# A two-lane attention GRU on one core: increments accumulated in PSUM, a bf16 score product for the shift, and DVE summing the exponentials

## The reference, cut to what matters

```python
def step(h, x_t):
    score = tanh([h ; enc] @ W_att)          # 77 x 128
    attn = softmax(score @ V_att)            # over the 77 context rows
    inp = [x_t ; attn @ enc]
    gz, gr, gh = split(inp @ Wi + b)
    rz, rr, rh = split(h @ Uh)
    z, r = sigmoid(gz + rz), sigmoid(gr + rr)
    hh = tanh(gh + r * rh)
    h_new = z * h + (1 - z) * hh
x = x + all h_new                            # x_t is layernorm(x)
```

## Time and profile before

| | us |
|---|---|
| median of 3 executions (4578.97 to 4592.61) | 4579.9 |
| span of the profiled execution, first to last instruction | 4575.7 |
| the profiled execution's own time | not given beside its span |
| recurrence in it, first to last write of h | 256.0 to 2283.5 |

### The profile page before, as it was taken

How to read it: one execution, slowest core, us unless ns; L and a number is a source line. 1 busy time by engine, 2 the same in 40 slices (tenths; PEclk the granted TensorE clock), 3 DMA queues, 4 the chain that set the end, 5 groups by cost and what they waited for, 6 DMA issues and landing times. The chain is left out here.

```text
span 4575.7 us, 82192 instructions
## 1 busy us (share of the span) xinstructions
PE 4041.4 (88%) x25247; PEld 2348.8 (51%) x25308; DVE 2805.4 (61%) x13508; ACT 2308.3 (50%) x6560; POOL 948.4 (21%) x4509
## 2 busy tenths in 40 slices
PE   7889999999999999999899999778888888888868
PEld 2367777777777777777733334322333333333222
DVE  3466666666666666666654454546666666666534
ACT  5355565555555555555533334214555555555423
POOL 0323333333333333333331000300000000100002
PEclk9999999999999999999999999758888888888879
DMA  0100000000000000000001000011111111111100
GB/s 9 56 2 2 2 2 2 2 2 2 2 2 2 2 2 2 2 2 2 6 31 37 1 1 1 22 57 45 45 57 45 57 57 45 57 52 49 33 30 5
DMA packets 48838, 94.48 MB, mean 21 GB/s; under 512 B 11296, under 2 KB 31792, under 8 KB 48144
## 3 DMA queue, kind: packets, MB, share of 16 engines
q1 hardware_dynamic: 48400, 89.22, 6.0%
HBM read 72.88 MB, written 15.39 MB: 19 GB/s over the span
## 5 line engine op out<-in xcount | busy, mean ns | idle before, releaser
L939 PE MATMUL ps<-g_h,w_p 128*128 128x128 f32 x4096 | 918.2, 306 | 0.0
L2280 ACT ACTIVATE t_ex<-ps 128x1024 f32<-128x1024 f32 (+1 forms) x480 | 471.8, 1021 | 571.8 <-PE ps L2227 558.1
L939 PEld LDWEIGHTS ps<-g_h,w_p 128*128 128x128 f32 x4096 | 616.7, 190 | 0.0
L935 PE MATMUL ps<-g_h,w_p 128*128 128x77 f32 x2048 | 456.5, 304 | 174.5 <-DVE g_h L1009 145.9
L2375 DVE TENSOR_REDUCE t_ncol<-ps 128x1 f32<-128x512 f32 x768 | 486.6, 685 | 154.6 <-PE ps L2200 154.0
L1005 DVE SCALAR_TENSOR_TENSOR g_used<-g_encg,g_e 128x77 f32<-128x77 f32 x3072 | 550.3, 230 | 0.0
L975 ACT ACTIVATE g_th<-ps 128x77 f32<-128x77 f32 x1024 | 241.4, 236 | 535.5 <-PE ps L935 535.5
L1051 POOL TENSOR_SCALAR g_z<-g_tzr 128x1 f32<-128x1 f32 x1024 | 194.7, 190 | 1363.0 <-ACT g_tzr L984 1363.0
L935 PEld LDWEIGHTS ps<-g_h,w_p 128*128 128x128 f32 x2048 | 304.5, 188 | 310.3 <-DVE g_h L1009 295.5
L956 PE MATMUL ps<-g_th,g_vrep 128*128 128x77 f32 x2048 | 456.6, 305 | 0.0
L1014 DVE TENSOR_REDUCE g_ntop<-ps 128x1 f32<-128x77 f32 x1024 | 244.1, 238 | 338.2 <-PE ps L956 337.3
(11 more groups left out here) (481 smaller groups left out, 6910.3 us busy)
## 6 DMA issues: line engine op xcount, KB each, us to landing
t_qst<-t_turn_q SPq DMA_DIRECT2D x288, 96.0 KB
t_kst<-t_turn_k SPq DMA_DIRECT2D x144, 96.0 KB
t_turn_q<-t_part SPq DMA_DIRECT2D x24, 384.0 KB, 2.5
t_turn_k<-t_part SPq DMA_DIRECT2D x12, 384.0 KB, 3.3
t_wf<-in_t_wf SPq DMA_DIRECT2D x6, 514.5 KB, 5.5
m_experts<-in_experts SPq DMA_DIRECT2D x1, 3072.0 KB, 12.7
t_wa<-in_t_wa SPq DMA_DIRECT2D x6, 448.0 KB, 3.4
t_wx<-in_t_wx SPq DMA_DIRECT2D x6, 448.0 KB, 4.2
```

Source lines behind the costliest of these rows:

```text
L935: M(att[c], w["att_h"], h[t % 2][:, c:c + 1].broadcast_to([P, S]), start=False, stop=True, skip_group_check=True).then_inc(*st.sem("att", c))
L939: return M(G[c][:, g], weights, h[t % 2][:, c:c + 1].broadcast_to([P, P]), start=False, stop=last, skip_group_check=True)
L2280: A(ex[0:kw, slot[pf, c, l, n]], ps[0:kw, at:at + 2], ACT.Exp, scale=SCALE).then_inc(*st.sem(f"{pf}e{n}", c))
```

## The change

- PE's operand is no longer h but its increment dh. The attention sum (`att`) and the gate sums (`gates`) are not opened anew at each step: they stay in PSUM, and each step adds W times dh to all 128 columns of a gate at once. Column t of the bank, which was filled with `gx` of 128 tokens by float32 identity products (`fill`), then holds the gate of token t. Once in 128 steps the banks are opened again from the full h (`hist`).
- r's and z's products both stand ahead of `scores`, the candidate's behind; the bf16 opening products are gone.
- `rough` is a new single bf16 product: the upper halves of tanh's float32 values times V in bf16. `top` takes the maximum from it, while exp still reads the float32 `score`.
- exp loses its accumulator output. DVE gets `sum`, a reduction of e over 77 columns, waits for it before the reciprocal, and `hm` moves behind `zr`.
- `update` makes dh = (hh - h) * (1 - z) on DVE. POOL keeps 1 - z and adds dh to the history, and drops z, z * h, the save and the splitting. DVE adds the whole history to x at the end.

```diff
...
-        gx = sb("gx", [P, B, T, 3])
+        gx = sb("gx", [P, B, 3, T])
...
-        gxs = sb("gxs", [P, 3, B, T, 3], BF16)
-        encs = sb("encs", [P, 3, B, S], BF16)
+        zero = sb("zero", [P, 1])
...
-        h = [sb(f"h{i}", [P, B]) for i in range(2)]
+        vrepb = sb("vrepb", [P, P], BF16)
+        hist = sb("hist", [P, B, T + 1])
+        dh = [sb(f"dh{i}", [P, B]) for i in range(2)]
...
+        SPAN = P
+        att = [ps[:, 4 * c, 0:S] for c in range(B)]
+        score = [ps[:, 4 * c + 1, 0:S] for c in range(B)]
+        rough = [ps[:, 4 * c + 3, 0:S] for c in range(B)]
+        upper = [th[:, c].bitcast(BF16).rearrange("p (s h) -> p s h", h=2)[:, :, 1] for c in range(B)]
+
+        gates = [ps[:, 4 * c + 2, 0:3 * SPAN].rearrange("p (g n) -> p g n", n=SPAN) for c in range(B)]
+        plain = [ps[:, 4 * c + 2, 3 * SPAN:3 * SPAN + 1] for c in range(B)]
...
-                def open_att(c):
-                    for i in range(3):
-                        M(att[c], identb[:], encs[:, i, c], start=(i == 0), stop=False, skip_group_check=True)
+                def moved(c, t, n):
+
+                    a = hist[:, c, t:t + 1] if t % SPAN == 0 else dh[t % 2][:, c:c + 1]
+                    return a.broadcast_to([P, n])
 
                 def attend(c, t):
-                    if t:
-                        pe.wait_ge(*st.at("h", c, t - 1))
-                    M(att[c], w["att_h"], h[t % 2][:, c:c + 1].broadcast_to([P, S]), start=False, stop=True,
-                      skip_group_check=True).then_inc(*st.sem("att", c))
...
+                    if t % SPAN == 0:
+                        if t:
+                            pe.wait_ge(*st.at("h", c, t - 1))
+                        M(att[c], k.ident[:], encp[:, c], start=True, stop=False, skip_group_check=True)
+                    else:
+                        pe.wait_ge(*st.at("dh", c, t - 1))
+                    M(att[c], w["att_h"], moved(c, t, S), start=False, stop=True, skip_group_check=True).then_inc(*st.sem("att", c))
+
+                def fill(c, t):
+                    for g in range(3):
+                        M(gates[c][:, g], k.ident[:], gx[:, c, g, t:t + SPAN], start=(g == 0), stop=False, skip_group_check=True)
+                    M(plain[c], k.ident[:], zero[:], start=False, stop=False, skip_group_check=True)
+
+                def recur(c, t, g):
+                    return M(gates[c][:, g], w["uh"][:, g * D:(g + 1) * D], moved(c, t, SPAN), start=False, stop=False,
                              skip_group_check=True)
...
-                def open_gates(c, t):
-                    if t and t % SLICE == 0 and c == 0:
-                        pe.wait_ge(sliced, SPLIT * (t // SLICE + 1))
-                    for i in range(3):
-                        M(G[c][:, :, 0], identb[:], gxs[:, i, c, t:t + 1].rearrange("p o g -> p (o g)"),
-                          start=(i == 0), stop=False, skip_group_check=True)
-                    recur(c, t, 1, w["uh"][:, D:2 * D])
-
-                def close_gates(c, t):
-                    recur(c, t, 0, w["uh"][:, 0:D])
-                    recur(c, t, 2, uhh[:], last=True).then_inc(*st.sem("gates", c))
+                def recur_candidate(c, t):
+                    M(ps[:, 4 * c + 2, 2 * SPAN:3 * SPAN + 1], uhh[:], moved(c, t, SPAN + 1), start=False, stop=True,
+                      skip_group_check=True).then_inc(*st.sem("gates", c))
 
                 def scores(c, t):
                     pe.wait_ge(*st.at("tanh", c, t))
-                    M(score[c], vrep[:], th[:, c], start=True, stop=True).then_inc(*st.sem("score", c))
-
-                for c in range(B):
-                    open_att(c)
+                    M(rough[c], vrepb[:], upper[c], start=True, stop=True, skip_group_check=True).then_inc(*st.sem("rough", c))
+                    M(score[c], vrep[:], th[:, c], start=True, stop=True, skip_group_check=True).then_inc(*st.sem("score", c))
+
                 for t in range(T):
                     for c in range(B):
                         attend(c, t)
-                        open_gates(c, t)
+                        if t % SPAN == 0:
+                            fill(c, t)
+                        recur(c, t, 1)
+                        recur(c, t, 0)
                         scores(c, t)
-                        close_gates(c, t)
-                        if t + 1 < T:
-                            open_att(c)
+                        recur_candidate(c, t)
...
                 def exp(c, t):
+                    act.wait_ge(*st.at("score", c, t))
                     act.wait_ge(*st.at("top", c, t))
-                    A(e[:, c], score[c], ACT.Exp, bias=ntop[:, c:c + 1], accum_out=esum[:, c:c + 1])\
+                    A(e[:, c], score[c], ACT.Exp, bias=ntop[:, c:c + 1])\
                         .then_inc(*st.sem("exp", c))
...
-                    A(hh[:, c:c + 1], G[c][:, 2, 1:2], ACT.Tanh, bias=hin[:, c:c + 1], scale=tzr[:, c, 1:2])\
+                    A(hh[:, c:c + 1], plain[c], ACT.Tanh, bias=hin[:, c:c + 1], scale=tzr[:, c, 1:2])\
...
                 def top(c, t):
-                    dve.wait_ge(*st.at("score", c, t))
-                    V.tensor_reduce(ntop[:, c:c + 1], score[c], AX, ALU.max, negate=True).then_inc(*st.sem("top", c))
+                    dve.wait_ge(*st.at("rough", c, t))
+                    V.tensor_reduce(ntop[:, c:c + 1], rough[c], AX, ALU.max, negate=True).then_inc(*st.sem("top", c))
 
                 def mix(c, t):
                     dve.wait_ge(*st.at("exp", c, t))
+                    V.tensor_reduce(esum[:, c:c + 1], e[:, c], AX, ALU.add).then_inc(*st.sem("sum", c))
+                    weigh("r", 1, c)
+                    dve.wait_ge(*st.at("sum", c, t))
                     V.reciprocal(sinv[:, c:c + 1], esum[:, c:c + 1]).then_inc(*st.sem("sinv", c))
-                    weigh("r", 1, c)
                     weigh("z", 0, c)
-                    weigh("hm", 2, c)
                     dve.wait_ge(*st.at("gates", c, t))
                     dve.wait_ge(*st.at("z", c, t))
-                    fma("zr", c, zr[:, c], mac[:, c, 0:2], sinv[:, c:c + 1], G[c][:, 0:2, 0])
+                    fma("zr", c, zr[:, c], mac[:, c, 0:2], sinv[:, c:c + 1], gates[c][:, 0:2, t % SPAN])
+                    weigh("hm", 2, c)
                     dve.wait_ge(*st.at("hm", c, t))
-                    fma("in", c, hin[:, c:c + 1], mac[:, c, 2:3], sinv[:, c:c + 1], G[c][:, 2, 0:1])
+                    fma("in", c, hin[:, c:c + 1], mac[:, c, 2:3], sinv[:, c:c + 1], gates[c][:, 2, t % SPAN:t % SPAN + 1])
...
                 def update(c, t):
-                    if t >= 2:
-                        dve.wait_ge(*st.at("saved", c, t - 2))
-                    dve.wait_ge(*st.at("zh", c, t))
+                    if t:
+                        dve.wait_ge(*st.at("h", c, t - 1))
+                    dve.wait_ge(*st.at("omz", c, t))
                     dve.wait_ge(*st.at("cand", c, t))
-                    fma("h", c, h[1 - t % 2][:, c:c + 1], hh[:, c:c + 1], omz[:, c:c + 1], zh[:, c:c + 1])
+                    V.scalar_tensor_tensor(out=dh[1 - t % 2][:, c:c + 1], in0=hh[:, c:c + 1], scalar=hist[:, c, t:t + 1],
+                                           in1=omz[:, c:c + 1], op0=ALU.subtract, op1=ALU.mult).then_inc(*st.sem("dh", c))
...
+                for c in range(B):
+                    dve.wait_ge(*st.at("h", c, T - 1))
+                    V.tensor_tensor(k.x[:, c], k.x[:, c], hist[:, c, 1:T + 1], ALU.add).then_inc(summed, 1)
+                dve.wait_ge(summed, B)
...
-                def factors(c, t):
+                def factor(c, t):
                     pool.wait_ge(*st.at("tzr", c, t))
-                    nc.gpsimd.tensor_scalar(z1[:, c:c + 1], tzr[:, c, 0:1], 0.5, 0.5, ALU.mult, ALU.add).then_inc(*st.sem("z1", c))
                     nc.gpsimd.tensor_scalar(omz[:, c:c + 1], tzr[:, c, 0:1], -0.5, 0.5, ALU.mult, ALU.add).then_inc(*st.sem("omz", c))
-                    pool.wait_ge(*st.at("z1", c, t))
-                    nc.gpsimd.tensor_tensor(zh[:, c:c + 1], z1[:, c:c + 1], h[t % 2][:, c:c + 1], ALU.mult).then_inc(*st.sem("zh", c))
...
-                def save(c, t):
-                    pool.wait_ge(*st.at("h", c, t))
-                    at = k.x[:, c, t:t + 1]
-                    nc.gpsimd.tensor_tensor(at, at, h[1 - t % 2][:, c:c + 1], ALU.add).then_inc(*st.sem("saved", c))
...
+                def advance(c, t):
+                    pool.wait_ge(*st.at("dh", c, t))
+                    nc.gpsimd.tensor_tensor(hist[:, c, t + 1:t + 2], hist[:, c, t:t + 1], dh[1 - t % 2][:, c:c + 1], ALU.add)\
+                        .then_inc(*st.sem("h", c))
 
                 for t in range(T):
                     for c in range(B):
-                        if t:
-                            save(c, t - 1)
-                        factors(c, t)
-                    split_next(t)
+                        factor(c, t)
+                        advance(c, t)
...
```

(28 more changed lines are left out.)

18 lines of the change are left out of this document (4 added, 14 removed).

## The result

| | before | after |
|---|---|---|
| median of 4 executions, us | 4584.6 (4578.97 to 4592.61) | 4644.7 (4642.61 to 4647.69) |
| span of the profiled execution, us | 4575.7 | 4645.9 |
| steps in it, first to last, us | 256.0 to 2283.5 | 264.8 to 2351.3 |
| average step (over 511.5), us | 3.964 | 4.079 |

The ratio of after to before is 1.0133, 95% interval [1.0119, 1.0147]: slower by 60 us, where 26 us faster was forecast. The time lies inside the range; the sign is wrong.

A forecast was written before the change was run, and what follows sets the result against it. Bound before: one lane's latency chain, 3.964 us a step; after: the lanes' alternation, 3.88 + 0.02 = 3.90, so -33 us; +6 for bank reopenings, +1 at the end, total -26: 4554 us on the median, range 4500 to 4650.

The forecast's parts named there:

- The bound moves to the alternation: Lanes sharing DVE and ACT in fixed order: two halves of 1.94 make 3.88 a step, above the lane's chain of 3.77.
- dh for h: End of a lane's step: dh follows hh by 0.48, without the wait for POOL's product, minus 0.08.
- The shift: Scores to exp: top from one bf16 product lets exp start at about 0.57 instead of 0.76, minus 0.19.
- The sum on DVE: Exp to reciprocal: sum 0.36 after exp's start, r at 0.155, reciprocal 0.16 after r.
- z to zr at 0.27: On DVE, zr directly behind z needs z's accumulator: read ends 0.24 after z's start, with the handover 0.27.
- The stretched steps at 0.02: Recurrence: a few stretched steps add 0.02 to the average step, 3.88 + 0.02 = 3.90.
- the boundaries of 128 steps: Reopening the banks once in 128 steps: 1.5 us each, four times, +6 us (3 to 9).
- a clock under full speed: Sign that the forecast is wrong: TensorE's clock below full in the recurrence, now that PE has fewer products.
- Accumulators come later than recorded: Rival, 28%: z to zr and hm to `in` cost up to 0.15 more per half; 4708 us, midway 4631.
- z to zr over 0.29: Sign in the timeline on DVE, pointing to the slower rival.
- Waits on own results cost little: Rival, 15%: zr 0.155 behind z, `in` 0.155 behind hm; 4380 us in full, 4442 mild, 4498 likeliest.
- The bf16 product brings nothing: Rival, 7%: operand read in steps of two, top no earlier than now; lane 3.97, +20 us, 4600.

The follow-up runs named there:

- a7: The kernel before with the increments in PSUM alone (ScalarE's sum, hm ahead of zr, shift from the float32 score): 4548.4 us, ratio 0.9927 to before.
- b1: The kernel before with the bf16 product and the shift from it, nothing else: 4497.4 us, ratio 0.9821 to before.
- a1: The kernel after with DVE's wait for the gates moved from directly ahead of zr to the front of the mix: 4625.4 us, ratio 1.0082 to before.
- a2: The kernel after with a second, always satisfied wait for the gates added ahead of `in`: 4742.0 us, ratio 1.0342 to before.
- a8: The kernel after with three more, unused bf16 products of 77 columns on PE in each lane-step: 4628.1 us, ratio 1.0108 to before.
- b2: The kernel before with the new end of the step alone (sum on DVE, zr ahead of hm): 4630.5 us, ratio 1.0107 to before.
- a5: The kernel after with the sum back in ScalarE's accumulator and hm back ahead of zr: 4464.1 us, ratio 0.9749 to before.

## Why the prediction was wrong

- **The bound moves to the alternation: right.** hh to the other lane's exp is 0.25 in 979 of 1023 cases, and top comes 0.37 ahead of exp.
- **dh for h, the waits for POOL gone: right.** hh to dh 0.49 (0.48 forecast). Increments alone brought 32 us (a7).
- **The shift: right in size.** Alone it brought 83 us (b1); 0.19 a step less for the lane was forecast, 97 us.
- **The sum on DVE: right.** dh to sum 0.14, sum to r 0.14 (0.155), to the reciprocal 0.15 (0.16), exp to sum 0.38 where 0.36 stood; the other lane's round binds.
- **z to zr at 0.27: the term that failed.** It is 0.34. The forecast took it to be the same wait as hm to `in`, which was right at 0.27. But zr has two waits ahead of it. a1 moves one away and gets 0.26 (median); a2 adds one at `in` and gets 0.36. The term could be read in the kernel before: in the step of the earlier trace rows zr starts 0.20 behind z's read (1005.76 to 1005.96), exactly as in after, with hm in between. The forecast built its 0.27 from the record of the read and a handover instead, and took the 0.36 from z to zr in the earlier trace rows for an upper bound of its rival alone. It never asked how many waits a step has. Twice 0.07 less the hundredths won elsewhere turn 3.88 into 4.00: 512 x 0.12 = 61 us.
- **The stretched steps at 0.02: too small.** Measured 4.079 - 4.00 = 0.08, and the boundaries of 128 steps among them: 40 us, where 10 for the stretched steps and 6 for the boundaries stood, 24 more. Some 15 of these go with the clock (a8). The prediction named a clock under full speed as a sign, and gave it no price.
- **The sum:** -26 forecast, 61 and 24 more make +59; measured +60.

**The rivals.** "Accumulators come later than recorded" has the time (4631 in its middle form) and its sign, z to zr over 0.29, but not its cause: hm to `in` is on time. It asked for two late places and there is one, for another reason: the second wait. "Waits on own results cost little" is out: an operation that waits for its neighbour starts 0.12 after the start of the read, one that doesn't starts with it. The Trainium skill, page VectorE: DVE Perf Modes, section "The DRAIN you can't avoid", has it of a chain of eight copies that a semaphore after each costs nothing extra; for the short operations here the trace disagrees, where the reader of an accumulator starts 0.12 behind the start of its read with one awaited semaphore and 0.20 with two, and an operation that doesn't need it starts with the read. "The bf16 product brings nothing" is out by b1.

What b2 and a5 show beyond it: with zr ahead of hm the kernel would have been slower than a5 even at the forecast 0.27 (3.88 a step by the forecast, about 3.70 in a5). The change's two other parts are worth 116 us, and its end took all of them and some 60 more.

## What to carry to other kernels

Where a short operation reads what the same engine has just made, put an independent operation between the two: hm in that place was worth 137 us, at no cost in work. Count the waits ahead of each instruction on the path, not only the operations, and place those that are long satisfied where the engine idles anyway. When an operation is to be moved out from between two others, look how far apart these two already are: that distance may stay. When lanes alternate on in-order engines, add up the round that they share as well as the chain of one: a gain in the chain is worth little (24 of 83 us here) once the round is longer.
